# Routing's inverse by one-hots: the tile's one-hot moved to GpSimd, the weighted biases added by VectorE straight from PSUM

## The chip, the cores and the metric

One core of one Trainium2 chip runs the kernel. The metric is the device time of one launch in microseconds (us). The engines are named as in the profile: PE (TensorE), PEld (its weight loads), DVE (VectorE), ACT (ScalarE), POOL (GpSimd) and SP (SyncE, which only issues DMAs here).

## The reference, cut to what matters

A layer of attention with a post-layernorm, then a mixture of experts with a post-layernorm, for 4 x 1024 tokens of 256 numbers:

```python
x = _layernorm(x + attention(x, W_in, b_in, W_out, b_out))
raw_gate = softmax(x @ gate)                      # 16 experts
_, topk_idx = top_k(raw_gate, 3)
gate_topk = mask * raw_gate / max(sum(abs(mask * raw_gate)), 1e-12)
hidden = relu(x @ W1[e] + b1[e])                  # every expert e
expert_out = hidden @ W2[e] + b2[e]
x = _layernorm(x + sum_e gate_topk[e] * expert_out[e])
```

The part `sum_e gate_topk[e] * b2[e]` is the weighted bias of a token. It does not depend on the experts' matmuls and is added to `x` while the routing is worked out.

## The kernel before

Four stages run one after the other, each a block that begins and ends with a barrier of all engines: attention, routing (`routing_phase`), experts, combine. The change lies in routing alone.

Routing holds the 4096 tokens as `TILES` = 32 tiles of 128 rows in `x1`. After the layernorm and the gate, DVE picks the three experts of every token and works out, for each pair of a token and one of its `TOPK` = 3 experts, a slot: the slots of an expert are next to each other and filled up to tiles of 128, `SLOT_TILES` = 112 tiles in all. The expert stage gathers tokens by slot, so the map from pairs to slots has to be inverted. That is done with one-hot matrices on PE. For each of the 96 pairs of tile and choice (i = 3t + k):

- DVE compares the iota row `ioq` with `row_of` (the slot's row, per token): `row_hot`, 128 x 128 in bf16 (L1216).
- DVE compares the same iota with `tile_of` (the slot's tile) and multiplies with the token's row number plus 1, `part`: `tile_hot`, 128 x 112 in bf16 (L1218).
- ACT makes `row_hot_k`, that is `row_hot` times 4t + k + 1 (L1095).
- PE adds `row_hot`^T `tile_hot` into `inv_ps` (L1035) and `row_hot_k`^T `tile_hot` into a bank of `tr_ps` (L1038). Both sums run over all 96 pairs.

Each of the three one-hots has a ring of `HOT` = 8 buffers, handed back by PE through the semaphore `r_inv` (L1038). The rings lie in the memory of the tile `oh`, which is the name the profile gives them. Every sixth pair DVE also does one small instruction for `etile`, the expert of each slot tile (L1224, L1227). When all 96 pairs are done, DVE turns the two sums into the index lists `src_i` and `dst_i` (L1237 to L1252), and the barrier follows.

The weighted biases use the same engines. For each tile t, PE multiplies the gate weights `gT` with the 16 rows of `b2r` (32 rows of the array, f32, L1023) into one of two banks, `lg_ps` or `bb_ps` in turn. ACT copies the bank to `biases`, which lies in `xtt` (L1085), and POOL adds it to `x1` (L951). The first `EARLY_BIASES` = 10 tiles are done before the loop over the 96 pairs, on PE and ACT, while DVE works out the slots. The other 22 stand in the loop, one after every fourth pair.

What sets the order: each engine works through its own instructions in the order of the code, and semaphores tie them together. Nothing is scheduled by a program. Routing's stores of `x1` to memory (`r_stored`) must be done before `x1` is added to.

Of the kernel before, what the change touches and what calls it, by code (L numbers as in the profile page):

```python
# [7 lines left out]
ALU = mybir.AluOpType  # L8
# [9 lines left out]
B, T, D = 4, 1024, 256  # L18
# [803 lines left out]
def routing_phase(nc, A, dram, S):  # L822
# [5 lines left out]
    with ExitStack() as ctx:  # L828
        def sb(name, shape, dt):
# [6 lines left out]
        stats = sb("stats", [P, TILES, 6], F32)  # L836
        mv = sb("mv", [P, TILES, 2], F32)
        r = [sb(f"ln_{i}", [P, TILES], F32) for i in range(5)]
        EARLY_BIASES = 10
        HOT = 8  # L840
        LG = 8
        BY_POOL = 5
# [30 lines left out]
        unused = sb("unused", [P, SLOT_TILES], F32)  # L873
        ioq = sb("ioq", [P, P], BF16)

        biases = xtt[:, :, 0:D]
        g32 = xtt[:].rearrange("p a (t e) -> p (a t) e", e=32)
        ef = sb("ef", [1, SLOT_TILES], F32)
        eps = sb("eps", [P, 1], F32)
# [9 lines left out]
        inv_ps = ctx.enter_context(nc.psum_tensor("inv_ps", [P, 512], F32))  # L889
        bb_ps = ctx.enter_context(nc.psum_tensor("bb_ps", [P, 512], F32))  # L890
        x1_in = [ctx.enter_context(nc.semaphore(f"x1_in{b}")) for b in range(B)]
        names = ("r_slots r_ef r_oh r_oh_a r_oh_k r_bb_sb r_inv r_stored r_bb r_bbadd r_w r_small r_const r_chain "
                 "r_ln r_var r_std r_x1 r_xtr r_xtt r_lg r_lt r_lgt r_vo r_b1 r_bout r_bias_p r_bias_v r_rs r_sub "
                 "r_exp r_mask r_pre r_g32 r_gtr r_gt r_b2z r_b2").split()
        m = {k: ctx.enter_context(nc.semaphore(k)) for k in names}
# [23 lines left out]
        @block.gpsimd  # L919
        def _(pool):  # L920
            pool.memset(b2r[:], 0.0).then_inc(m["r_b2z"], 1)
            pool.memset(tri[:], 1.0).then_inc(m["r_const"], 1)
            pool.memset(ones[:], 1.0).then_inc(m["r_const"], 1)
            pool.memset(zero[:], 0.0).then_inc(m["r_const"], 1)
            pool.iota(io16[:], pattern=[[1, E_]], base=0, channel_multiplier=0,
                      allow_small_or_imprecise_dtypes=True).then_inc(m["r_const"], 1)
            pool.iota(iot[:], pattern=[[1, SLOT_TILES]], base=0, channel_multiplier=0,
                      allow_small_or_imprecise_dtypes=True).then_inc(m["r_const"], 1)
            pool.memset(onesf[:], 1.0).then_inc(m["r_const"], 1)
            pool.memset(ident[:], 0.0).then_inc(m["r_const"], 1)  # L930
            for t, pattern, base, mult in ((ioq, [[1, P]], 0, 0), (unused, [[P, SLOT_TILES]], PLACES * NTOK + P, 1),
                                           (part, [[0, 1]], 1, 1)):
                pool.iota(t[:], pattern=pattern, base=base, channel_multiplier=mult,
                          allow_small_or_imprecise_dtypes=True).then_inc(m["r_const"], 1)
            pool.wait_ge(m["r_const"], 10)
            pool.affine_select(out=ident[:], in_=ident[:], compare_op=ALU.not_equal, fill=1.0, base=0,
                               pattern=[[-1, P]], channel_multiplier=1).then_inc(m["r_const"], 1)

            pool.affine_select(out=tri[:], in_=tri[:], compare_op=ALU.is_gt, fill=0.0, base=0,
                               pattern=[[1, P]], channel_multiplier=-1).then_inc(m["r_const"], 1)  # L940

            pool.wait_ge(m["r_bout"], 1)
            for g in range(0, TILES, LG):
                pool.wait_ge(x1_in[g // LG], 16)
                for t in range(g, g + BY_POOL):
                    nc.gpsimd.tensor_tensor(x1[:, t, :], x1[:, t, :], bout[:], ALU.add).then_inc(m["r_bias_p"], 1)

            pool.wait_ge(m["r_stored"], 16 * TILES // LG)
            for t in range(TILES):
                pool.wait_ge(m["r_bb_sb"], t + 1)  # L950
                nc.gpsimd.tensor_tensor(x1[:, t, :], biases[:, t % 2, :], x1[:, t, :], ALU.add)\  # L951
                    .then_inc(m["r_bbadd"], 1)

        @block.tensor
        def _(pe):
# [62 lines left out]
            def weighted_biases(t):  # L1018

                if t >= 2:  # L1020
                    pe.wait_ge(m["r_bb_sb"], t - 1)
                r0 = 32 * (t % 4)
                nc.tensor.matmul((lg_ps, bb_ps)[t % 2][:, 0:D], gT[r0:r0 + 32, (t // 4) * P:(t // 4 + 1) * P],  # L1023
                                 b2r[r0:r0 + 32, :], start=True, stop=True).then_inc(m["r_bb"], 1)
# [6 lines left out]
                weighted_biases(t)  # L1031
            last = TOPK * TILES - 1
            for i in range(last + 1):
                pe.wait_ge(m["r_oh"], i + 1)
                nc.tensor.matmul(inv_ps[:, 0:SLOT_TILES], row_hot[:, i % HOT, :], tile_hot[:, i % HOT, :],  # L1035
                                 start=(i == 0), stop=(i == last), skip_group_check=True)
                pe.wait_ge(m["r_oh_k"], i + 1)
                nc.tensor.matmul(tr_ps[:, 0, 0:SLOT_TILES], row_hot_k[:, i % HOT, :],  # L1038
                                 tile_hot[:, i % HOT, :], start=(i == 0), stop=(i == last),
                                 skip_group_check=True).then_inc(m["r_inv"], 1)  # L1040
                if i % 4 == 0 and EARLY_BIASES + i // 4 < TILES:
                    weighted_biases(EARLY_BIASES + i // 4)

        @block.scalar
        def _(act):
            def take_logits(v):
                act.wait_ge(m["r_lg"], 2 * v + 2)
                if v >= 2:
                    act.wait_ge(m["r_lgt"], v - 1)
                nc.scalar.activation(lt_sb[v % 2][0:E_, :], lt_ps[v % 2][0:E_, :], ACT.Copy).then_inc(m["r_lt"], 1)  # L1050

            def take_transposes(u):

                act.wait_ge(m["r_xtr"], u + 1)
                if u >= 2:
                    act.wait_ge(m["r_lg"], u - 1)
                nc.scalar.activation(xtt[:, u % 2, :], tr_ps[:, u % 2, :], ACT.Copy).then_inc(m["r_xtt"], 1)
                if u >= 2 and u % 2 == 0:
                    take_logits(u // 2 - 1)

            for g in range(TILES // LG):

                ts = slice(g * LG, (g + 1) * LG)
                act.wait_ge(m["r_var"], g + 1)
                nc.scalar.activation(r[0][:, ts], mv[:, ts, 1], ACT.Sqrt, bias=eps[:, 0:1]).then_inc(m["r_std"], 1)
                act.wait_ge(m["r_rs"], g + 1)
                for t in range(g * LG, (g + 1) * LG):
                    nc.scalar.activation(x1[:, t, :], x1[:, t, :], ACT.Identity, bias=r[4][:, t:t + 1],
                                         scale=r[3][:, t:t + 1]).then_inc(m["r_x1"], 1)
                    if g >= 1 and t % 2 == 1:  # L1070
                        take_transposes((t - LG) // 2)
            for u in range((TILES - LG) // 2, TILES // 2):
                take_transposes(u)
            take_logits(TILES // 4 - 1)
            act.wait_ge(m["r_sub"], 1)
            nc.scalar.activation(prob[:], tmp[:], ACT.Exp).then_inc(m["r_exp"], 1)
            for u in range(2):
                act.wait_ge(m["r_gtr"], u + 1)
                nc.scalar.activation(gT[:, 512 * u:512 * u + 512], tr_ps[:, u, :], ACT.Copy).then_inc(m["r_gt"], 1)

            def take_biases(t):
                act.wait_ge(m["r_bb"], t + 1)
                if t >= 2:
                    act.wait_ge(m["r_bbadd"], t - 1)
                nc.scalar.activation(biases[:, t % 2, :], (lg_ps, bb_ps)[t % 2][:, 0:D], ACT.Copy)\  # L1085
                    .then_inc(m["r_bb_sb"], 1)

            for t in range(EARLY_BIASES):
                take_biases(t)
            for i in range(TOPK * TILES):  # L1090
                t, k = i // TOPK, i % TOPK
                act.wait_ge(m["r_oh_a"], i + 1)
                if i >= HOT:
                    act.wait_ge(m["r_inv"], i - HOT + 1)
                nc.scalar.activation(row_hot_k[:, i % HOT, :], row_hot[:, i % HOT, :], ACT.Copy,  # L1095
                                     scale=float(PLACES * t + k + 1)).then_inc(m["r_oh_k"], 1)
                if i % 4 == 3 and EARLY_BIASES + i // 4 < TILES:
                    take_biases(EARLY_BIASES + i // 4)

        @block.vector  # L1100
        def _(dve):
# [107 lines left out]
            V.tensor_copy(row_of[:], sloti[:, 1])  # L1209
            V.tensor_copy(tile_of[:], sloti[:, 2]).then_inc(m["r_slots"], 1)  # L1210
            dve.wait_ge(m["r_slots"], 1)
            for i in range(TOPK * TILES):
                t, k = i // TOPK, i % TOPK
                if i >= HOT:
                    dve.wait_ge(m["r_inv"], i - HOT + 1)
                V.tensor_scalar(row_hot[:, i % HOT, :], ioq[:], row_of[:, k, t:t + 1], None, ALU.is_equal)\  # L1216
                    .then_inc(m["r_oh_a"], 1)
                V.tensor_scalar(tile_hot[:, i % HOT, :], ioq[:, 0:SLOT_TILES], tile_of[:, k, t:t + 1],  # L1218
                                part[:, 0:1], ALU.is_equal, ALU.mult).then_inc(m["r_oh"], 1)
                if i % (TOPK * TILES // E_) == 0:  # L1220

                    e = i // (TOPK * TILES // E_)
# [422 lines left out]
```

## Time and profile before

| | us |
|---|---|
| median of 3 runs | 2046.22 |
| lowest and highest of them | 2040.72, 2048.99 |
| the profiled execution | 2043.57 |
| its span in the trace | 2041.8 |
| mean granted clock of PE over the span | 0.921 of full speed |
| the loop over the 96 pairs, first DVE start to last PE end | 1480.88 to 1533.01 |
| routing's last stretch, slots worked out to barrier | 1470.8 to 1538 |

The span is the time between the first and the last instruction in the trace, and the profiled execution's own time is 1.8 us longer. The busy tenths of the page show the three large stages: attention to about slice 27 of 40, routing in slices 28 to 30, experts and combine behind. PE busy time includes waiting in its pipeline, so a busy PE is not PE at its peak.

### The profile page before, as it was taken

To read this page: it belongs to the slowest core of one execution; us is meant where nothing else is said; L and a number is where in the kernel's file an instruction comes from. 1 tells how busy PE (TensorE), PEld (TensorE's weight loads), DVE (VectorE), ACT (ScalarE), POOL (GpSimd) and SP (SyncE) were. 2 spreads that over 40 slices of the span, in tenths; PEclk is the share of its full clock that TensorE was granted. 3 is DMA by queue.
4 is the path that set the end of the run, shared out by engine and by line. 5 is a ranking of instruction groups with operands and counts; after the bars stand their busy time and mean duration, and the time that the engine had idled before them with its cause. 6 is when DMAs were issued, how large, how long until landed. Compare 5 with 4: busy or idle time off the path is not lost. (4 is left out here: it accounts for less than half of the span.)

```text
span 2041.8 us, 37021 instructions
## 1 busy us (share of the span) xinstructions
PE 1796.5 (88%) x10191; PEld 1326.3 (65%) x10193; DVE 1403.8 (69%) x2857; ACT 763.1 (37%) x1691; POOL 1181.2 (58%) x1086
## 2 busy tenths in 40 slices
PE   4489999998998998999998999983598999999940
PEld 3366676666666765666675667642257999999940
DVE  3378878876886886887876887756694444444438
ACT  3134444443443443443443444433361222122225
POOL 2256776775676765766775677563134555555544
PEclk9689999998998998999999999996758999999975
DMA  9775566564555644654665456408601222222255
GB/s 319 243 203 146 154 187 177 156 188 136 153 171 156 192 147 144 194 159 136 184 174 161 125 164 186 126 1 300 217 1 55 72 69 69 70 71 70 70 174 186
DMA packets 164547, 301.36 MB, mean 148 GB/s; under 512 B 18768, under 2 KB 57360, under 8 KB 163360
## 3 DMA queue, kind: packets, MB, share of 16 engines
q1 hardware_dynamic: 152608, 269.79, 44.2%
q0 software_dynamic: 10752, 29.37, 4.6%
q8 instruction: 73, 1.20, 0.3%
q14 instruction: 90, 0.74, 0.1%
q10 hardware_dynamic: 1024, 0.26, 0.1%
HBM read 192.15 MB, written 106.95 MB: 146 GB/s over the span
## 5 line engine op out<-in xcount | busy, mean ns | idle before, releaser
L686 ACT ACTIVATE prob<-b_ps 128x512 f32<-128x512 f32 (+3 forms) x768 | 357.2, 489 | 443.4 <-PE b_ps L531 349.2
L454 POOL TENSOR_TENSOR acc<-acc,prob 128x1024 f32<-128x1024 f32 (+1 forms) x192 | 351.1, 1828 | 26.2 <-issue 22.7
L530 PE MATMUL b_ps<-q,k 128*128 128x512 f32 (+3 forms) x768 | 316.0, 416 | 36.2 <-issue 32.2
L755 DVE TENSOR_REDUCE max_b<-a_ps 128x1 f32<-128x512 f32 (+3 forms) x512 | 283.7, 570 | 87.3 <-PE a_ps L519 32.4
L427 POOL TENSOR_TENSOR roped<-rot 128x512 f32<-128x512 f32 x128 | 174.4, 1363 | 217.0 <-DVE rot L768 216.3
L519 PE MATMUL a_ps<-k,q 128*128 128x512 f32 (+3 forms) x768 | 276.4, 390 | 18.0 <-DMA k<-scratch_hilo 9.0
L604 PE MATMUL y_ps<-prob,v_sb 128*64 128x512 f32 (+3 forms) x1536 | 274.3, 492 | 0.0
L531 PE MATMUL b_ps<-q,k 65*128 65x512 f32 (+3 forms) x768 | 268.7, 354 | 0.0
L1410 DVE TENSOR_SCALAR hT<-h_ps,b1T 128x128 f32<-128x128 f32 x448 | 126.1, 344 | 190.7 <-PE h_ps L1329 171.6
L794 DVE RECIPROCAL inv<-inv 128x128 f32<-128x128 f32 x256 | 231.8, 927 | 7.7 <-ACT inv L718 7.0
L432 POOL TENSOR_TENSOR lo<-roped,hi 128x512 fp32r<-128x512 f32 x128 | 177.8, 1389 | 85.1 <-ACT hi L699 85.1
L1329 PEld LDWEIGHTS h_ps<-mxT,w_now 128*128 128x128 f32 x1792 | 219.0, 193 | 6.6 <-ACT mxT L1369 1.0
L604 PEld LDWEIGHTS y_ps<-prob,v_sb 128*64 128x64 f32 x1536 | 105.1, 137 | 180.6 <-issue 175.7
L1329 PE MATMUL h_ps<-mxT,w_now 128*128 128x128 f32 x1792 | 219.6, 276 | 0.6 <-ACT mxT L1369 0.6
L530 PEld LDWEIGHTS b_ps<-q,k 128*128 128x128 f32 x768 | 151.6, 197 | 94.8 <-issue 74.2
L1338 PE MATMUL yo_ps<-w,hT 128*128 x896 | 211.8, 379 | 0.0
L1303 POOL DMA_INDIRECT scratch_ys<-y,dst_i x112 | 110.8, 989 | 172.4 <-ACT y L1376 164.5
L511 PE MATMUL g_ps<-xT,w_sb 128*128 128x512 f32 x768 | 194.0, 403 | 9.6 <-DVE rot L768 6.6
L440 POOL TENSOR_SCALAR_AFFINE_SELECT prob<-prob 128x256 f32<-128x256 f32 x256 | 113.5, 449 | 149.5 <-ACT prob L686 147.1
L519 PEld LDWEIGHTS a_ps<-k,q 128*128 128x128 f32 x768 | 153.3, 200 | 42.3 <-DVE max_b L755 11.3
L511 PEld LDWEIGHTS g_ps<-xT,w_sb 128*128 128x128 f32 x768 | 147.9, 196 | 41.3 <-DVE rot L768 7.3
L1338 PEld LDWEIGHTS yo_ps<-w,hT 128*128 128x128 f32 x896 | 161.5, 190 | 17.4
(248 smaller groups left out, 2712.8 us busy)
## 6 DMA issues: line engine op xcount, KB each, us to landing
q<-scratch_hilo SPq DMA_DIRECT2D x192, 256.0 KB, 4.3
k<-scratch_hilo SPq DMA_DIRECT2D x192, 256.0 KB, 5.2
scratch_hilo<-hi SPq DMA_DIRECT2D x64, 512.0 KB, 4.1
scratch_hilo<-lo SPq DMA_DIRECT2D x64, 512.0 KB, 4.8
w_sb<-scratch_wsplit SPq DMA_DIRECT2D x32, 512.0 KB, 3.5
w<-in_L_ffn_W_dram SPq DMA_DIRECT2D x32, 512.0 KB, 10.4
got<-scratch_ys SPq DMA_DIRECT2D x32, 384.0 KB, 6.9
wv_sb<-scratch_wsplit SPq DMA_DIRECT2D x16, 512.0 KB, 6.3
```

What stands on the lines that cost most here:

```text
L432: nc.gpsimd.tensor_tensor(lo[:, half, cs], roped[:], hi[:, half, cs].bitcast(F32), ALU.subtract).then_inc(m["lo_done"], 1)
L454: nc.gpsimd.tensor_tensor(sums, old, probs(q), ALU.add).then_inc(m["sum_p"], 1)
L511: ins = nc.tensor.matmul(out, left, right, start=(a, b, k) == PRODUCTS[0], stop=(a, b, k) == PRODUCTS[-1], skip_group_check=True)
L519: ins = nc.tensor.matmul(out, q1[s][:, h, blk * P:(blk + 1) * P], k1[s][:, h, k0:k0 + w], start=True, stop=not diagonal, skip_group_check= ...
L530: nc.tensor.matmul(out, k1[s][:, h, js], q1[s][:, h, qs], start=True, stop=False, skip_group_check=True)
L531: ins = nc.tensor.matmul(out, k2[s][0:65, h, js], q2[s][0:65, half, h, 512 - w:512], start=False, stop=True, skip_group_check=True)
L604: ins = nc.tensor.matmul(y_ps[64 * h:64 * h + 64, 512 - w:512], v_sb[:, pairs, j, s, 64 * h:64 * h + 64], probs(q)[:, h, :], start=(j == 0 ...
L686: nc.scalar.activation(probs(q)[:, h, :], b_ps[:, h, 0:w], ACT.Exp).then_inc(exp_done[h], 1)
L755: nc.vector.tensor_reduce(out, a_ps[:, h, 0:w], AX_X, ALU.max, negate=True).then_inc(a_max[h], 1)
L794: nc.vector.reciprocal(part, part).then_inc(inv_done[c], 1)
L1329: ins = nc.tensor.matmul(h_ps[:, s, c * P:(c + 1) * P], w1_now[:, s, k, c * P:(c + 1) * P], xT[:, s, k * P:(k + 1) * P], start=(k == 0), s ...
L1338: ins = nc.tensor.matmul(yo_ps[:, s, 0:D], hT[:, s, c * P:(c + 1) * P], w2[:, bass.ds(e, 1), c, :].rearrange("p a d -> p (a d)"), start=(c ...
```

## The change

- POOL builds `tile_hot` (L952 of the changed kernel), with the same operations and ring as DVE did. It waits for `r_slots` once, and for its ring through `r_inv`. DVE keeps `row_hot` alone.
- DVE adds the weighted bias of tile t to `x1`, reading the bank in PSUM (L1207). It does so after `row_hot` of the tile's third pair (k = 2). ACT's copy and POOL's add of every tile are gone, and so is the semaphore `r_bb_sb` between them. PE now waits for the add (`r_bbadd`) before it writes a bank again.
- `EARLY_BIASES` goes from 10 to 2, and the other 30 stand in PE's stream one after every third pair.
- PE waits for both DVE's `row_hot` (`r_oh_a`) and POOL's `tile_hot` (`r_oh`) before the first of a pair's matmuls. The wait for the stores (`r_stored`) goes from POOL to DVE.

```diff
-        EARLY_BIASES = 10
+        EARLY_BIASES = 2
...
-            pool.wait_ge(m["r_stored"], 16 * TILES // LG)
-            for t in range(TILES):
-                pool.wait_ge(m["r_bb_sb"], t + 1)
-                nc.gpsimd.tensor_tensor(x1[:, t, :], biases[:, t % 2, :], x1[:, t, :], ALU.add)\
-                    .then_inc(m["r_bbadd"], 1)
+            pool.wait_ge(m["r_slots"], 1)
+            for i in range(TOPK * TILES):
+                t, k = i // TOPK, i % TOPK
+                if i >= HOT:
+                    pool.wait_ge(m["r_inv"], i - HOT + 1)
+                nc.gpsimd.tensor_scalar(tile_hot[:, i % HOT, :], ioq[:, 0:SLOT_TILES], tile_of[:, k, t:t + 1],
+                                        part[:, 0:1], ALU.is_equal, ALU.mult).then_inc(m["r_oh"], 1)
...
-                    pe.wait_ge(m["r_bb_sb"], t - 1)
+                    pe.wait_ge(m["r_bbadd"], t - 1)
...
             for i in range(last + 1):
+                pe.wait_ge(m["r_oh_a"], i + 1)
                 pe.wait_ge(m["r_oh"], i + 1)
...
-                if i % 4 == 0 and EARLY_BIASES + i // 4 < TILES:
-                    weighted_biases(EARLY_BIASES + i // 4)
+                if i % TOPK == TOPK - 1 and EARLY_BIASES + i // TOPK < TILES:
+                    weighted_biases(EARLY_BIASES + i // TOPK)
...
-            for t in range(EARLY_BIASES):
-                take_biases(t)
...
-                if i % 4 == 3 and EARLY_BIASES + i // 4 < TILES:
-                    take_biases(EARLY_BIASES + i // 4)
...
+            dve.wait_ge(m["r_stored"], 16 * TILES // LG)
+
+            def add_biases(t):
+                dve.wait_ge(m["r_bb"], t + 1)
+                V.tensor_tensor(x1[:, t, :], (lg_ps, bb_ps)[t % 2][:, 0:D], x1[:, t, :], ALU.add)\
+                    .then_inc(m["r_bbadd"], 1)
...
-                V.tensor_scalar(tile_hot[:, i % HOT, :], ioq[:, 0:SLOT_TILES], tile_of[:, k, t:t + 1],
-                                part[:, 0:1], ALU.is_equal, ALU.mult).then_inc(m["r_oh"], 1)
+                if k == 2:
+                    add_biases(t)
```

PE's stream where the loop begins, before (10 biases ahead of it, of which the last two are shown, then one after the first pair and one after the fifth; `inv_ps` and `tr_ps` are the two sums):

```order
1525 L1023 MATMUL lg_ps<-b2r,gT 128x256
1526 L1023 MATMUL bb_ps<-b2r,gT 128x256
1527 L1035 MATMUL inv_ps<-oh 128x112
1528 L1038 MATMUL tr_ps<-oh 128x112
1529 L1023 MATMUL lg_ps<-b2r,gT 128x256
1530 L1035 MATMUL inv_ps<-oh 128x112
1531 L1038 MATMUL tr_ps<-oh 128x112
1532 L1035 MATMUL inv_ps<-oh 128x112
1533 L1038 MATMUL tr_ps<-oh 128x112
1534 L1035 MATMUL inv_ps<-oh 128x112
1535 L1038 MATMUL tr_ps<-oh 128x112
1536 L1035 MATMUL inv_ps<-oh 128x112
```

The same place of PE's stream after the change:

```order
1517 L1024 MATMUL lg_ps<-b2r,gT 128x256
1518 L1024 MATMUL bb_ps<-b2r,gT 128x256
1519 L1037 MATMUL inv_ps<-oh 128x112
1520 L1040 MATMUL tr_ps<-oh 128x112
1521 L1037 MATMUL inv_ps<-oh 128x112
1522 L1040 MATMUL tr_ps<-oh 128x112
1523 L1037 MATMUL inv_ps<-oh 128x112
1524 L1040 MATMUL tr_ps<-oh 128x112
1525 L1024 MATMUL lg_ps<-b2r,gT 128x256
1526 L1037 MATMUL inv_ps<-oh 128x112
1527 L1040 MATMUL tr_ps<-oh 128x112
```

Only two biases are left ahead of the loop, and one follows every three pairs instead of every four.

DVE's stream some way into the loop, before (the two one-hots of each pair in turn, L1227 every sixth pair):

```order
778 L1218 TENSOR_SCALAR oh<-ioq,tile_of,part 128x112
779 L1227 SCALAR_TENSOR_TENSOR ef<-iot,cnt,ef 1x112
780 L1216 TENSOR_SCALAR oh<-ioq,row_of 128x128
781 L1218 TENSOR_SCALAR oh<-ioq,tile_of,part 128x112
782 L1216 TENSOR_SCALAR oh<-ioq,row_of 128x128
783 L1218 TENSOR_SCALAR oh<-ioq,tile_of,part 128x112
```

DVE's stream there after the change (L1214 is `row_hot`, L1207 the add of a weighted bias):

```order
778 L1207 TENSOR_TENSOR x<-bb_ps,x 128x256
779 L1214 TENSOR_SCALAR oh<-ioq,row_of 128x128
780 L1225 SCALAR_TENSOR_TENSOR ef<-iot,cnt,ef 1x112
781 L1214 TENSOR_SCALAR oh<-ioq,row_of 128x128 x2
782 L1207 TENSOR_TENSOR x<-lg_ps,x 128x256
783 L1214 TENSOR_SCALAR oh<-ioq,row_of 128x128 x3
784 L1207 TENSOR_TENSOR x<-bb_ps,x 128x256
```

The tile's one-hot of every pair is gone from it, and an add from PSUM came in after every third pair.

## Rows read from the trace of the kernel before

**Rows 1.** The page: span, busy times of the engines, and the granted clock in 40 slices

```profile
span 2041.8 us, 37021 instructions
PE 1796.5 (88%) x10191; PEld 1326.3 (65%) x10193; DVE 1403.8 (69%) x2857; ACT 763.1 (37%) x1691; POOL 1181.2 (58%) x1086
PEclk9689999998998998999999999996758999999975
```

**Rows 2.** Busy time by stretch: gate, early biases, the loop over pairs, tail

```profile
core 0: us, PE busy (x) PEld busy (x) DVE busy (x) ACT busy (x) POOL busy (x), PEclk, DMA share, GB/s
1420.50:1447.00 26.50, 23.79 (x137) 12.00 (x136) 6.49 (x32) 19.97 (x41) 0.00 (x0) 1.00 1.07 366
1469.40:1480.80 11.40, 8.72 (x20) 4.25 (x20) 10.75 (x22) 3.72 (x10) 9.08 (x10) 0.50 0.01 1
1480.80:1533.00 52.20, 50.95 (x236) 28.22 (x236) 52.05 (x211) 33.47 (x118) 16.35 (x22) 0.50 0.00 1
1533.00:1538.00 5.00, 0.01 (x1) 0.00 (x0) 3.81 (x14) 0.00 (x0) 0.00 (x0) 0.50 0.00 0
```

**Rows 3.** DVE's timeline in the loop: start us, duration us, instruction

```profile
1500.04 0.23 DVE L1216 TENSOR_SCALAR oh<-ioq,row_of 128x128 bf16<-128x128 bf16 x1
1500.20 0.29 DVE L1218 TENSOR_SCALAR oh<-ioq,tile_of,part 128x112 bf16<-128x112 bf16 x1
1500.42 0.32 DVE L1227 SCALAR_TENSOR_TENSOR ef<-iot,cnt,ef 1x112 f32<-1x112 f32 x1
1500.66 0.76 DVE L1216 TENSOR_SCALAR oh<-ioq,row_of 128x128 bf16<-128x128 bf16 x1
1501.35 0.29 DVE L1218 TENSOR_SCALAR oh<-ioq,tile_of,part 128x112 bf16<-128x112 bf16 x1
```

**Rows 4.** POOL's timeline there

```profile
1500.66 0.72 POOL L951 TENSOR_TENSOR x<-xtt,x 128x256 f32<-128x256 f32 x1 [1.35 <-ACT xtt L1085]
```

**Rows 5.** PE's timeline there, around one weighted bias

```profile
1500.83 0.27 PE L1038 MATMUL tr_ps<-oh 128*128 128x112 bf16 x1
1501.03 1.22 PE L1023 MATMUL bb_ps<-b2r,gT 32*128 32x256 f32 x2
1502.18 0.27 PE L1035 MATMUL inv_ps<-oh 128*128 128x112 bf16 x1
1502.25 0.30 PE L1038 MATMUL tr_ps<-oh 128*128 128x112 bf16 x1
1502.34 0.30 PE L1035 MATMUL inv_ps<-oh 128*128 128x112 bf16 x1
1502.44 0.30 PE L1038 MATMUL tr_ps<-oh 128*128 128x112 bf16 x1
```

**Rows 6.** DVE's timeline ahead of the loop, the slots

```profile
1471.76 1.11 DVE L1200 TENSOR_TENSOR inc<-inc,cnt 128x512 f32<-128x512 f32 x1
1473.98 0.72 DVE L1204 TENSOR_TENSOR gtmp<-slots,oh 128x512 f32<-128x512 f32 x1
1475.45 1.07 DVE L1204 TENSOR_TENSOR gtmp<-slots,oh 128x512 f32<-128x512 f32 x1
1479.11 0.58 DVE L1206 CAST sloti<-slotf 128x96 int32<-128x96 f32 x1
1479.72 0.65 DVE L1207 TENSOR_SCALAR sloti<-sloti 128x96 int32<-128x96 int32 x1
1480.29 0.20 DVE L1208 TENSOR_SCALAR sloti<-sloti 128x96 int32<-128x96 int32 x1
1480.88 0.26 DVE L1216 TENSOR_SCALAR oh<-ioq,row_of 128x128 bf16<-128x128 bf16 x1
```

**Rows 7.** Groups by line and form, DVE, the whole of routing: busy us, mean ns

```profile
L1201 DVE TENSOR_TENSOR slots<-pre_ps,inc 128x512 f32<-128x512 f32 x1 | 1.0, 1041 | 0.0
L1181 DVE TENSOR_TENSOR xtt<-gtmp,red 128x512 f32<-128x512 f32 x1 | 0.7, 692 | 0.0
L1155 DVE TENSOR_TENSOR gtmp<-lg_ps,red 128x512 f32<-128x512 f32 x1 | 0.7, 690 | 0.0
L1240 DVE TENSOR_TENSOR tot<-tr_ps,tot 128x112 f32<-128x112 f32 x1 | 0.3, 274 | 0.0
```

**Rows 8.** Groups by line and form in the loop, ACT

```profile
L1095 ACT ACTIVATE oh<-oh 128x128 bf16<-128x128 bf16 x96 | 28.9, 307 | 19.5 <-DVE oh L1216 17.6
```

**Rows 9.** PE's timeline at the loop's start and end

```profile
1481.42 0.27 PE L1035 MATMUL inv_ps<-oh 128*128 128x112 bf16 x1 [2.55 <-DVE oh L1218]
...
1532.73 0.28 PE L1038 MATMUL tr_ps<-oh 128*128 128x112 bf16 x1
```

**Rows 10.** Groups by line and form, POOL, the whole span

```profile
L440 POOL TENSOR_SCALAR_AFFINE_SELECT prob<-prob 128x256 f32<-128x256 f32 x256 | 113.5, 449 | 149.5 <-ACT prob L686 147.1 <-issue 2.5
L454 POOL TENSOR_TENSOR acc<-acc,prob 128x512 f32<-128x512 f32 x32 | 41.3, 1290 | 0.0
L454 POOL TENSOR_TENSOR acc<-acc,prob 128x256 f32<-128x256 f32 x32 | 23.3, 729 | 25.6 <-issue 22.7 <-POOL acc L454 1.4
L939 POOL TENSOR_SCALAR_AFFINE_SELECT tri<-tri 128x128 bf16<-128x128 bf16 x1 | 0.3, 292 | 0.0
```

More of the change, by code:

```diff
@@ L874, in routing_phase @@
         ioq = sb("ioq", [P, P], BF16)
-        biases = xtt[:, :, 0:D]
         g32 = xtt[:].rearrange("p a (t e) -> p (a t) e", e=32)
@@ L891, in routing_phase @@
         x1_in = [ctx.enter_context(nc.semaphore(f"x1_in{b}")) for b in range(B)]
-        names = ("r_slots r_ef r_oh r_oh_a r_oh_k r_bb_sb r_inv r_stored r_bb r_bbadd r_w r_small r_const r_chain "
+        names = ("r_slots r_ef r_oh r_oh_a r_oh_k r_inv r_stored r_bb r_bbadd r_w r_small r_const r_chain "
                  "r_ln r_var r_std r_x1 r_xtr r_xtt r_lg r_lt r_lgt r_vo r_b1 r_bout r_bias_p r_bias_v r_rs r_sub "
@@ L1079, in _ @@
                 nc.scalar.activation(gT[:, 512 * u:512 * u + 512], tr_ps[:, u, :], ACT.Copy).then_inc(m["r_gt"], 1)
[L1081 to L1086, printed above, removed]
-            for t in range(EARLY_BIASES):
-                take_biases(t)
             for i in range(TOPK * TILES):
```

## The prediction

> **What bounds the kernel now.** I read the page first. PE is busy 88% of the span, and its granted clock stands near full speed except in slices 27 to 30 [rows 1]. The change touches only that place, so I read busy time by stretch there [rows 2]. In the loop over the 96 pairs DVE is busy 52.05 of 52.20 us. PE shows 50.95 us, at a granted clock of 0.50, the lower of its two levels (1.2 GHz). The loop's end is what the tail, the barrier and the experts wait for, and nothing else runs meanwhile: DMA share is 0.00. So a microsecond of the loop is a microsecond of the kernel.
>
> DVE's timeline tells what DVE's 52 us are [rows 3]. The row's one-hot starts at 1500.04, the tile's at 1500.20 and the next instruction at 1500.42, so a pair costs 0.38 us, though the durations are 0.23 and 0.29. L1227 costs 0.24. Then a row's one-hot takes 0.76 us instead of 0.23. POOL's add began in the same moment and took 0.72 us [rows 4]. DVE went on at 1501.35, where 1500.82 would have been due: 0.53 us lost to one POOL instruction. The sum: 96 x 0.38 + 16 x 0.24 + 22 x 0.53 = 36.5 + 3.8 + 11.7 = 52.0 us, which is the loop.
>
> The second thing to see is how close PE is behind [rows 5]. Inside the catch-up a pair costs PE 2 x 0.093 us. Around a bias the step from the matmul before it to the matmul behind it is 1500.83 to 1502.18, that is 1.35 us. This is PE's own time: the tile's one-hot that the matmul at 1502.18 needs had started at 1501.35 and took 0.29 [rows 3], so it had been there for half a microsecond. Four pairs and a bias therefore take PE 1.35 + 0.07 + 6 x 0.093 = 1.98 us, against DVE's 4 x 0.38 + 0.67 x 0.24 + 0.53 = 2.21 us. PE has only 10% of slack, and the change alters the mix on PE too.
>
> **The change part by part.**
>
> *Ahead of the loop.* Ten POOL adds ran beside DVE's slot arithmetic (9.08 us of POOL busy) [rows 2]; they go. What they cost DVE is read from twins: L1200 took 1.11 us, L1181 of the same form 0.69 (0.42 lost); the second of the three L1204 took 1.07, as did the third, the first 0.72 (2 x 0.35); L1206 took 0.58 and L1207 0.65 where L1208 took 0.20 (0.38 and 0.45) [rows 6, 7]. That is 1.95 us. L1201 took 1.04; against L1155, which also reads PSUM, 0.35 too much, but its second input is strided, so 0 to 0.35. I take 2.1 us. The loop then starts at 1480.88 - 2.1 = 1478.8.
>
> *DVE in the loop.* The tile's one-hot leaves: 96 x 0.22 us. The adds come in: L1155 (512 columns, PSUM) takes 0.690 and L1240 (112 columns, PSUM) 0.274, which makes 1.04 ns a column and 0.42 us for 256 [rows 7]. Three pairs cost DVE 3 x 0.17 to 0.22, plus 0.42, plus half of 0.24: 1.05 to 1.2 us, 34 to 38 us for the loop, before any hold by POOL.
>
> *ACT.* 32 copies go and the 96 of L1095 at 0.307 us stay, 29.5 us [rows 8]. ACT was not the bound and is not after.
>
> *PE in the loop.* Eight biases move in from ahead of the loop, where PE had nothing else to do and DVE covered them; inside, that cover is gone. Three pairs and a bias cost 1.35 + 0.07 + 4 x 0.093 = 1.79 us by rows 5, and 1.68 us if half of the 0.20 us ahead of a bias (1500.83 to 1501.03) turns out to have been waiting. The added wait on `r_oh_a` costs PE nothing as long as DVE is ahead. DVE can be: its add of tile j waits for a bias that PE issued two groups earlier, and it still leaves six pairs of row one-hots ready.
>
> The end by PE's pace: the first three pairs are fed at the makers' speed. First matmul at 1478.8 + 0.5 (as now, 1480.88 to 1481.42 [rows 6, 9]), first bias in the loop, which waits for DVE's first add behind three one-hots and L1222, at about 1480.6 (3 x 0.22 + 0.24 + 0.42, and two holds by POOL of 0.2 each). Then 29 groups of 1.79 = 51.9, the last bias 1.15, and six pairs 1.0 + 0.3: the last matmul ends at 1534.9. Now it ends at 1532.73 + 0.28 = 1533.0 [rows 9]. That is **+1.9 us**; with 1.68 a group, -1.3 us.
>
> *POOL in the loop.* Its one-hot has no row in the trace. From below: one input, no pointer scalars, 0.292 us for 128 columns and 0.449 for 256, so 1.23 ns a column and 0.27 us for 112. From above, among rows of elementwise work: two inputs, 0.729 us for 256 and 1.290 for 512, so 2.19 ns a column and 0.41 us for 112 [rows 10]. It reads one stream but does two operations and two per-token scalars, so I take 0.4 and keep 0.27 to 0.75 (the whole 256-column add) for the range. PE asks for a pair every 1.79 / 3 = 0.60 us.
>
> POOL and DVE hold one another: rows 3 and 4 show DVE held for the POOL instruction's length less about 0.2. If a POOL one-hot of 0.4 and a row one-hot (0.17 from start to start) exclude one another wholly, a pair costs 0.57 us, just under PE's 0.60. By the Trainium skill (SBUF — State Buffer, "Who interferes with whom") the pair of ports that DVE and GpSimd share is an exclusive lock for the whole instruction, taken by a DVE tensor_scalar in a two-port mode and not by an instruction with one SBUF input outside these. By that rule the adds from PSUM run beside POOL unhindered; rows 3 and 4 agree for the one-hots, and no row shows a PSUM add beside POOL.
>
> *Tail.* L1237 to L1252 and the barrier stay as they are.
>
> The sum: 2043.57 + 1.9 = 2045.5 us for an execution like the profiled one, which lay 2.65 us below the median. Against the median I predict **2048.1 us**. The work off DVE is real (some 15 us) but PE, at the lower clock and with 30 biases in the loop in place of 22, takes it all.
>
> **The rivals.**
>
> 1. *POOL becomes the bound (slower).* Decides from 0.60 us a pair on, that is from 0.43 us for POOL's one-hot if the two engines exclude one another, from 0.60 if not. Each 0.1 us above is 9.6 us. At 0.75 us a pair: 1478.8 + 72 + 0.6 = 1551.4, +18 us, 2064.6. For it: the instruction has two operations and two pointer scalars that no POOL row has. Against it: both rows of elementwise work end below 0.45. The Trainium skill (GPSIMD Engine Reference, 3.1) speaks against the move: GpSimd is about half as fast as VectorE at elementwise work, and branching on data costs some 12 cycles an element. An estimate from that figure, if the comparison is done so, is 1.1 us for 112 elements, and the loop would be 107 us, about 55 us longer; no row here shows such a cost. Chance 0.17 for more than 10 us, and 0.10 for 0.60 to 0.70 a pair, +3 to +10 us.
>
> 2. *PE's clock rises (faster).* In the gate stretch PE stands at 1.00 (2.4 GHz) at 23.79 us busy of 26.50, but in the loop at 0.50 with 50.95 of 52.20 [rows 2]. Should it rise, a bias and pairs go at about half the price (0.9 us a group), and the makers bind: 0.40 to 0.57 us a pair, 38 to 55 us. At 0.45: 1478.8 + 43.2 + 0.6 = 1522.6, -10 us, 2036. Against it: what PE does between two biases hardly changes in kind, and it was as good as always busy at 0.50 before. Chance 0.06, of which half is faster by over 0.5%.
>
> 3. *A bias costs PE less than 1.35 us (faster).* If the step were mostly waiting that has another cause, PE would keep up with DVE and POOL and the loop would fall to 0.45 to 0.5 us a pair, -5 to -10 us. Rows 3 and 5 speak against it, since the one-hot was ready. Chance 0.05, of which 0.02 beyond 0.5%.
>
> **How the numbers follow.** A measurement of this kernel tells about 0.5%, 10.2 us, from no change. The forecast has 0.62. Slower by over 0.5%: 0.17. Faster by over 0.5%: 0.03 + 0.02, rounded to 0.05. Within: 0.78. The range: below, -1.3 us by the cheaper group, and part of rivals 2 and 3 and the spread of the median (2040.72 at the lowest of three), 2040. Above, rival 1 up to 0.72 us a pair, +15 us, 2062. Some 0.07 is left out below and 0.12 above.
>
> **What would show it.** The first row one-hot about 2 us after the last slot casts, at 1478.8 rather than 1480.9. What stood as L1200, L1206 and L1207 at 0.69, 0.21 and 0.20 us. In the loop PE's own row: bias to bias 1.8 us, PE's idle time before its matmuls near nothing, clock 0.50. POOL's one-hot about 0.4 us and idle between, released by PE. Loop 55 to 57 us long. The prediction is wrong if POOL's one-hot shows over 0.5 us with PE waiting for `r_oh`, if PE's clock shows 1.00 in the loop, or if bias to bias is under 1.6 us.

## Result and profile after

| | before | after |
|---|---|---|
| median, 4 runs each | 2045.38 | 2064.31 |
| lowest and highest | 2040.72, 2048.99 | 2063.03, 2068.65 |
| span of the profiled execution | 2041.8 | 2061.7 |
| loop, first DVE start to last PE end | 1480.88 to 1533.01: 52.1 us | 1480.41 to 1554.05: 73.6 us |

The ratio is 1.0098, with a 95% interval of 1.0072 to 1.0124. The change makes the kernel slower by about 19 us. The forecast was 2048.1 us in a range of 2040 to 2062, so the result lies outside it. It lies near what rival 1 had given for a POOL pace of 0.75 us a pair: 2064.6.

Busy time by stretch, the changed kernel (ahead of the loop, loop, tail), answers to [rows 2]:

```profile
core 0: us, PE busy (x) PEld busy (x) DVE busy (x) ACT busy (x) POOL busy (x), PEclk, DMA share, GB/s
1469.40:1480.40 11.00, 2.13 (x9) 1.01 (x7) 10.25 (x24) 1.20 (x2) 0.00 (x0) 0.50 0.00 0
1480.40:1554.00 73.60, 61.39 (x252) 29.12 (x252) 36.46 (x146) 25.32 (x96) 73.08 (x96) 0.50 0.00 1
1554.00:1559.00 5.00, 0.05 (x1) 0.00 (x0) 3.81 (x14) 0.00 (x0) 0.00 (x0) 0.50 0.00 0
```

DVE's share of the loop fell from 52.05 to 36.46 us, as planned. POOL is busy 73.08 of 73.60 us. The clock of PE is 0.50 as before.

Groups by line and form in the loop, answering to [rows 7, 8, 10] (busy us, mean ns, idle before):

```profile
L952 POOL TENSOR_SCALAR oh<-ioq,tile_of,part 128x112 bf16<-128x112 bf16 x96 | 73.1, 774 | 68.7 <-DVE tile_of L1201 68.7
...
L1214 DVE TENSOR_SCALAR oh<-ioq,row_of 128x128 bf16<-128x128 bf16 x96 | 22.8, 288 | 0.0
...
L1207 DVE TENSOR_TENSOR x<-bb_ps,x 128x256 f32<-128x256 f32 x16 | 6.8, 424 | 21.0 <-PE bb_ps L1024 21.0
```

POOL's one-hot takes 0.774 us in the mean, 0.737 in the median. The only idle time before it is the 68.7 us ahead of the first; in the loop it never waits. From the first start to the last it does one every 0.762 us. The add from PSUM takes 0.424 us, as worked out.

DVE's timeline ahead of the loop, answering to [rows 6]:

```profile
1473.32 0.69 DVE L1191 TENSOR_TENSOR inc<-inc,cnt 128x512 f32<-128x512 f32 x1
...
1476.54 0.69 DVE L1195 TENSOR_TENSOR gtmp<-slots,oh 128x512 f32<-128x512 f32 x1
...
1479.43 0.21 DVE L1197 CAST sloti<-slotf 128x96 int32<-128x96 f32 x1
1479.68 0.21 DVE L1198 TENSOR_SCALAR sloti<-sloti 128x96 int32<-128x96 int32 x1
```

All are free of POOL's hold, at the lengths of their twins. The instruction ahead of L1191 starts at 1472.60 here and at 1471.04 before, so this execution came to routing 1.56 us later; the loop started 0.47 us earlier all the same, a gain of 2.03 us.

PE's timeline at the loop's end, with what it waited for, answering to [rows 9]:

```profile
1551.51 0.25 PE L1037 MATMUL inv_ps<-oh 128*128 128x112 bf16 x1 [0.27 <-POOL oh L952]
1551.56 0.30 PE L1040 MATMUL tr_ps<-oh 128*128 128x112 bf16 x1
1552.26 0.25 PE L1037 MATMUL inv_ps<-oh 128*128 128x112 bf16 x1 [0.41 <-POOL oh L952]
1552.31 0.30 PE L1040 MATMUL tr_ps<-oh 128*128 128x112 bf16 x1
1552.99 0.25 PE L1037 MATMUL inv_ps<-oh 128*128 128x112 bf16 x1 [0.38 <-POOL oh L952]
1553.04 0.30 PE L1040 MATMUL tr_ps<-oh 128*128 128x112 bf16 x1
1553.71 0.25 PE L1037 MATMUL inv_ps<-oh 128*128 128x112 bf16 x1 [0.38 <-POOL oh L952]
```

DVE has made its last one-hot at 1549.1, and PE takes one pair each time POOL delivers one, every 0.72 to 0.75 us. Inside the loop the list of waits tells it otherwise, and could mislead (waiting engine, whom for, us in total, times, longest):

```profile
DVE x L1207 <- PE bb_ps L1024: 21.0, 15, 1.5
...
PE inv_ps L1037 <- POOL oh L952: 10.7, 5, 9.3
PE inv_ps L1037 <- DVE oh L1214: 9.7, 31, 0.5
```

By it DVE waits for PE most (34.8 us with the 13.8 us of the other bank), PE waits for DVE 31 times, and for POOL only five times. PE now waits for two semaphores before a pair, and the profile names the one that came last. DVE, which is held back by its ring until PE has taken a pair, makes its next one-hot just after; that is a consequence of POOL's pace, or else it is the cause. Two theories had to be told apart.

- **Theory 1:** POOL's pace, 0.76 us a pair, sets the loop.
- **Theory 2:** the hand-overs between PE's biases and DVE's adds set it, and POOL only looks busy.

### The profile page after: what moved, and what is told of

It reads as the page before. It is cut to its first block and busy times, and to the rows that moved or that the text cites. A ratio compares the mean times of both kernels' runs of the same rounds, so it can differ in the third digit from the quotient of the medians.

```text
span 2061.7 us, 37056 instructions
## 1 busy us (share of the span) xinstructions
PE 1801.1 (87%) x10192; PEld 1325.2 (64%) x10193; DVE 1388.2 (67%) x2793; ACT 754.2 (37%) x1659; POOL 1229.8 (60%) x1150
## 5 line engine op out<-in xcount | busy, mean ns | idle before, releaser
L519 PEld LDWEIGHTS a_ps<-k,q 128*128 128x128 f32 x768 | 152.9, 199 | 43.5 <-DVE max_b L755 11.4
```

The costliest lines, as they stand in the source:

```text
L519: ins = nc.tensor.matmul(out, q1[s][:, h, blk * P:(blk + 1) * P], k1[s][:, h, k0:k0 + w], start=True, stop=not diagonal, skip_group_check= ...
```

## Experiments

Loop lengths below are from the first start of the row's one-hot on DVE to the end of PE's last matmul. PE's modelled end is its last start plus 0.3 us. Where a second time is given with "against", it is the kernel before, run again beside the experiment.

**The biases of the loop left out** (`e4`). The matmuls of PE and the adds of DVE for tiles 2 to 31 are left out, so the output lacks these biases.

```diff
-                if i % TOPK == TOPK - 1 and EARLY_BIASES + i // TOPK < TILES:
-                    weighted_biases(EARLY_BIASES + i // TOPK)
...
-                if k == 2:
+                if k == 2 and t < 2:
                     add_biases(t)
```

> The changed kernel without the 30 weighted biases of the loop (PE's matmuls and DVE's adds for tiles 2 to 31 are left out, so the output lacks them). Theory 1, POOL's pace of 0.76 us a pair sets the loop: it stays at 73 to 74 us. Theory 2, the hand-overs between PE's biases and DVE's adds set it, as the list of waits names them (DVE waits for PE 34.8 us in the loop): PE has only 0.19 us a pair left, and the loop falls to 45 us or less.

Measured: 2064.64 us in one run, loop 1480.2 to 1551.9, 71.7 us. The stretch in the trace:

```profile
1480.20:1551.90 71.70, 33.17 (x192) 13.04 (x192) 30.02 (x117) 29.14 (x96) 71.09 (x96) 0.50 0.00 1
```

PE lost nearly half of its busy time and DVE a fifth, and the loop kept POOL's length. Theory 2 falls. The 1.9 us that it did lose are POOL's: its start to start went from 0.762 to 0.741 us in the mean.

**Only the other part of the change: DVE builds both one-hots, POOL nothing** (`e1`).

```diff
-                pe.wait_ge(m["r_oh_a"], i + 1)
...
+                V.tensor_scalar(tile_hot[:, i % HOT, :], ioq[:, 0:SLOT_TILES], tile_of[:, k, t:t + 1],
+                                part[:, 0:1], ALU.is_equal, ALU.mult).then_inc(m["r_oh"], 1)
```

(and POOL's loop gone)

> One part of the change alone: DVE adds the biases from PSUM as in the changed kernel, with 2 early biases and 30 in the loop, but DVE also builds the tile's one-hot as before, and POOL does nothing. DVE's sum: 96 x 0.38 + 16 x 0.24 + 32 x 0.36 = 51.8 us with no hold by POOL; PE's pace by the prediction's sum 1.79 us a group, 53.7. Theory 1 (POOL alone made it slow): loop 53 to 56 us, time within 3 us of the kernel before. Theory 2 (the biases in the loop and DVE's adds made it slow): loop over 65 us, time 10 us or more above before.

Measured: 2047.84 us against 2043.83, ratio 1.0016 (0.9998 to 1.0033); loop 1479.5 to 1536.5, 57.0 us. Busy time in that stretch:

```profile
1479.50:1536.50 57.00, 56.34 (x252) 31.19 (x252) 53.41 (x242) 29.68 (x96) 0.00 (x0) 0.50 0.00 1
```

Theory 1 holds: without POOL's one-hot the loss of 1% is gone, and PE is the one that is busy throughout.

**POOL builds every second pair's tile one-hot** (`e2`).

```diff
+                if not (i % 2 == 0):
+                    continue
                 nc.gpsimd.tensor_scalar(tile_hot[:, i % HOT, :], ...
...
+                if i % 2 == 0:
+                    pe.wait_ge(m["r_oh_a"], i + 1)
+                    pe.wait_ge(m["r_oh"], i // 2 + 1)
+                else:
+                    pe.wait_ge(m["r_oh_d"], (i + 1) // 2)
```

(DVE builds the others and counts them on `r_oh_d`)

> The changed kernel, with POOL building the tile's one-hot only of every second pair and DVE that of the others. POOL then needs 48 x 0.76 = 37 us, DVE 96 x 0.17 + 48 x 0.22 + 4 + 11.5 = 42 us, so neither binds. Theory 1: the loop falls from 73.6 us to what PE's pace gives, 1.79 us a group of three pairs and a bias, 54 to 55 us in all; this measures the PE term of the prediction. If PE's step around a bias were partly waiting, 1.68 a group or less, it is 51 us or less. Theory 2 (hand-overs): stays over 65 us.

Measured: 2046.71 us, ratio 1.0011 (0.9995 to 1.0026); loop 1478.8 to 1536.3, 57.5 us. PE's timeline from one bias to the next:

```profile
1504.78 1.22 PE L1026 MATMUL bb_ps<-b2r,gT 32*128 32x256 f32 x2
1505.93 0.27 PE L1042 MATMUL inv_ps<-oh 128*128 128x112 bf16 x1
1505.99 0.30 PE L1045 MATMUL tr_ps<-oh 128*128 128x112 bf16 x1
1506.09 0.30 PE L1042 MATMUL inv_ps<-oh 128*128 128x112 bf16 x1
1506.18 0.30 PE L1045 MATMUL tr_ps<-oh 128*128 128x112 bf16 x1
1506.27 0.30 PE L1042 MATMUL inv_ps<-oh 128*128 128x112 bf16 x1
1506.37 0.30 PE L1045 MATMUL tr_ps<-oh 128*128 128x112 bf16 x1
1506.60 1.22 PE L1026 MATMUL lg_ps<-b2r,gT 32*128 32x256 f32 x2
```

1506.60 - 1504.78 = 1.82 us, with no wait in it, in every group that I read (the first bias starts at 1481.12, the last, 29 groups on, at 1533.90), and the same in the run with DVE alone. This is PE's pace that the forecast rested on (1.79). The 0.2 us ahead of a bias is there although nothing is awaited: 0.23 from 1506.37 to 1506.60. The loop is longer than the 54 to 55 us expected for this run, which were rounded down from the prediction's own sum, 1478.8 to 1534.9 = 56.1 us. It is 1.4 us longer than that sum: 0.03 x 29 = 0.9, and 0.5 at the start, where the first bias came 2.3 us after the loop's begin (1481.12), not 1.8.

**What POOL's 0.74 us consists of** (`m1`, and `m3` for widths). POOL gets extra instructions on scratch tiles in the 68.7 us in which it waits for the slots, four of each form, each waited for. `m1` has eight forms:

```diff
+            for _ in range(4):
+                nc.gpsimd.tensor_scalar(jb[:, 0:56], ioq[:, 0:56], part[:, 0:1], part[:, 0:1], ALU.is_equal, ALU.mult).then_inc(m["r_junk"], 1)
+                pool.wait_ge(m["r_junk"], JUNK())
```

> The changed kernel with 32 extra POOL instructions, four of each of eight forms, each waited for, on scratch tiles in the 68 us in which POOL waits for the slots. The kernel's time should not change by more than 1 us, since POOL is idle there for 68.7 us. Question: what of the 737 ns of POOL's one-hot is what. Theory A, pointer scalars cost: the forms with immediates take about 0.3 us, the one with two per-token scalars 0.74, the one with one about 0.5. Theory B, the second operation costs: one-operation forms about 0.3 to 0.4 whatever the scalars. Theory C, the comparison costs (a branch or a select per element): add and multiply with the same scalars about 0.4, all comparing forms near 0.7. Theory D, a fixed price of the instruction: 56 columns take nearly the 0.74 us of 112. If it is all per column, 56 columns take about 0.43.

Measured: 2065.27 us in one run. Each line below gives the shortest, the median and the longest of its four instructions in ns. A per-token scalar is a value that the instruction reads from memory for each row, as the one-hot reads `tile_of` and `part`; a constant stands in the instruction. L956: compare, then multiply, two per-token scalars; L974 the same in f32; L959 on 56 columns; L965 the same with two constants; L971 add and multiply, two per-token scalars; L962 compare alone, one per-token scalar; L968 compare alone with a constant; L977 multiply alone with a constant.

```profile
L956 POOL TENSOR_SCALAR jb<-ioq,part x4: 737/738/754, 1411.9 to 1414.4; 128x112 bf16<-128x112 bf16 x4
L974 POOL TENSOR_SCALAR jf<-iot,part x4: 737/738/743, 1428.8 to 1431.4; 128x112 f32<-128x112 f32 x4
L959 POOL TENSOR_SCALAR jb<-ioq,part x4: 552/574/1097, 1415.2 to 1417.8; 128x56 bf16<-128x56 bf16 x4
L965 POOL TENSOR_SCALAR jb<-ioq x4: 587/588/592, 1421.1 to 1423.1; 128x112 bf16<-128x112 bf16 x4
L971 POOL TENSOR_SCALAR jb<-ioq,part x4: 428/434/1050, 1426.1 to 1428.3; 128x112 bf16<-128x112 bf16 x4
L962 POOL TENSOR_SCALAR jb<-ioq,part x4: 560/561/562, 1418.4 to 1420.4; 128x112 bf16<-128x112 bf16 x4
L968 POOL TENSOR_SCALAR jb<-ioq x4: 486/488/524, 1423.7 to 1425.5; 128x112 bf16<-128x112 bf16 x4
L977 POOL TENSOR_SCALAR jb<-ioq x4: 487/488/497, 1432.2 to 1433.9; 128x112 bf16<-128x112 bf16 x4
```

Two forms have one instruction of about twice the length of the other three. Both ran beside adds of DVE with two inputs from SBUF (the output bias onto `x1`). The third of L959 started at 1416.60, the first of L971 at 1426.08:

```profile
1416.27 1.08 DVE L1151 TENSOR_TENSOR x<-x,bout 128x256 f32<-128x256 f32 x3
1425.90 1.09 DVE L1151 TENSOR_TENSOR x<-x,bout 128x256 f32<-128x256 f32 x3
```

So the means of these two forms (0.699 and 0.586 us) mislead, and the medians are read here.

The comparison is the largest single item. With the one-hot's two per-token scalars, compare and multiply takes 0.74 us (L956) and add and multiply 0.43 (L971), so theory C's "about 0.4" for the add came true, and the comparison costs 0.30 us more. It does not do so everywhere: alone and with a constant, a compare takes what a multiply does, 0.49 us (L968, L977), so "all comparing forms near 0.7" is wrong. Theory A falls as the whole cause, since the add with two per-token scalars is the cheapest form of all; so does theory B, since that form has two operations. Among the comparing forms a per-token scalar adds 0.07 us (L962 over L968), and a multiply behind it 0.10 (L965 over L968). Half the columns save 0.18 us (L959 under L956), so theory D holds in part: three quarters of the time stay at 56 columns. Why the comparison is dear together with a second operation and two per-token scalars, and not alone, these runs do not show.

`m3` has other widths and kinds:

> The changed kernel with POOL instructions of other widths and kinds on scratch tiles in its idle stretch, four of each: the one-hot's operations over 336 and 224 columns; tensor_tensor adding over 112 and 336 columns and multiplying over 112, all bf16. From the first look at forms, 0.74 us at 112 columns and 0.70 at 56 make 0.77 ns a column and a fixed 0.66 us: 336 columns should take 0.91 us and 224 0.83. If the fixed part belongs to tensor_scalar alone, tensor_tensor at 112 columns takes 0.41 us by the slope of the prediction (2.19 ns a column), and 0.9 at 336.

Measured: 2068.61 us in one run, whose routing began some 5 us later than in the changed kernel's; its loop is 73.1 us long. L958 and L961 are the one-hot's operations, L967 and L964 tensor_tensor adding, L970 multiplying (shortest, median and longest in ns):

```profile
L958 POOL TENSOR_SCALAR jb<-jc,part x4: 1484/1492/1610, 1414.9 to 1419.7; 128x336 bf16<-128x336 bf16 x4
L961 POOL TENSOR_SCALAR jb<-jc,part x4: 1110/1112/1112, 1421.4 to 1425.0; 128x224 bf16<-128x224 bf16 x4
L967 POOL TENSOR_TENSOR jb<-jc x4: 758/784/884, 1428.0 to 1430.7; 128x336 bf16<-128x336 bf16 x4
L970 POOL TENSOR_TENSOR jb<-jc x4: 372/372/434, 1431.5 to 1433.0; 128x112 bf16<-128x112 bf16 x4
L964 POOL TENSOR_TENSOR jb<-jc x4: 371/371/372, 1426.2 to 1427.6; 128x112 bf16<-128x112 bf16 x4
```

The 0.91 us expected at 336 columns was wrong because it came from the mean of the 56-column form, with its one long instruction. By the shortest of each width, 0.552, 0.737, 1.110 and 1.484 us at 56, 112, 224 and 336 columns, the one-hot's form costs 3.3 ns a column throughout and 0.37 us besides. tensor_tensor costs 0.37 us at 112 columns, near the 0.41 that the prediction had worked out as its bound from above. The one-hot's tensor_scalar costs twice that; a tensor_scalar that adds and multiplies, 0.43, does not. A tensor_tensor that compares was planned as well (`m2`), but no run shows one.

**POOL and DVE side by side** (`e6`): half the tile one-hots on POOL, and the loop's biases left out as in `e4`, so the output lacks them.

> The kernel with the tile's one-hot shared half and half between POOL and DVE, without the 30 weighted biases of the loop (PE's matmuls and DVE's adds of tiles 2 to 31 are left out). It shows what the one-hots alone cost. DVE: 96 x 0.165 + 48 x 0.22 + 16 x 0.24 = 30.2 us, POOL 48 x 0.75 = 36 us. If the two engines run side by side, the loop is 36 to 38 us, POOL's; if POOL's instruction holds DVE for its length less 0.2 us, as the 128x256 add did in the kernel before, DVE needs 30 + 48 x 0.55 = 56 us and the loop is over 50.

Measured: 2028.75 us in one run, loop 1477.7 to 1518.4, 40.7 us. Busy time in that stretch:

```profile
1477.70:1518.40 40.70, 25.53 (x192) 15.41 (x192) 35.08 (x164) 26.39 (x96) 39.88 (x48) 0.50 0.01 1
```

Groups by line and form there:

```profile
L954 POOL TENSOR_SCALAR oh<-ioq,tile_of,part 128x112 bf16<-128x112 bf16 x48 | 39.9, 844 | 68.6 <-DVE tile_of L1204 68.6
...
L1217 DVE TENSOR_SCALAR oh<-ioq,row_of 128x128 bf16<-128x128 bf16 x96 | 23.4, 286 | 3.5 <-PE tr_ps L1045 2.3
```

The two run nearly side by side. DVE's row one-hot takes 0.286 us in the mean beside POOL's one-hot, where the 256-column add had made it 0.76 [rows 3, 4]. POOL pays more: its one-hot goes from 0.74 to 0.844, which makes the loop longer than the 36 to 38 us expected. Its last two instructions, which start when DVE has done its last one-hot, take 0.737 us each. By the Trainium skill (SBUF — State Buffer, "Who interferes with whom") the lock would be held for the whole instruction. The trace agrees with that for the add (0.72 us of POOL, 0.53 lost by DVE), but not for this one-hot: POOL was busy 39.88 of the 40.70 us, and DVE made 144 one-hots in them. What sets the two cases apart (POOL's operation, its number of inputs, its type) is not shown.

**Biases in twos.** Ahead of the loop of the kernel before, and nowhere inside it, biases stand directly one after another, and there two were done 1.2 us after they began. So the loop's biases are issued two at a time, in the kernel with half on POOL (`e3`), with all on DVE (`e7`), and with a third on POOL (`e8`).

```diff
-                if i % TOPK == TOPK - 1 and EARLY_BIASES + i // TOPK < TILES:
-                    weighted_biases(EARLY_BIASES + i // TOPK)
+                if i % 6 == 5 and EARLY_BIASES + i // 3 < TILES:
+                    weighted_biases(i // 3 + 1)
+                    weighted_biases(i // 3 + 2)
```

> The kernel with the tile's one-hot shared between POOL and DVE (every second pair each), and the weighted biases of the loop issued two at a time after every sixth pair instead of one after every third. In the run before, PE's step from bias to bias was 1.82 us in each group and set the loop, 57.5 us. Two biases back to back use different row groups of the array: ahead of the loop in the kernel before, the first two were both done 1.2 us after they began. Theory 1 (PE's price per bias binds): six pairs and two biases cost PE about 1.1 + 1.6 us in place of 3.6, and the loop falls to DVE's pace, 44 to 48 us; with the 2 us ahead of the loop the time is 6 to 10 us below the kernel before. Rival: two biases in a row cost twice one, nothing changes, loop 57 us.

Measured: 2039.3 us against 2043.59, ratio 0.9983 (0.9972 to 0.9995); loop 1481.9 to 1531.3, 49.4 us. PE's timeline:

```profile
1503.62 0.79 PE L1026 MATMUL lg_ps<-b2r,gT 32*128 32x256 f32 x1
1503.63 0.79 PE L1026 MATMUL bb_ps<-b2r,gT 32*128 32x256 f32 x1
1504.21 0.63 PE L1026 MATMUL lg_ps<-b2r,gT 32*128 32x256 f32 x1
1504.22 0.63 PE L1026 MATMUL bb_ps<-b2r,gT 32*128 32x256 f32 x1
1504.78 0.27 PE L1042 MATMUL inv_ps<-oh 128*128 128x112 bf16 x1
```

A bias is two records in this view, in `e2` shown as x2. The two biases start 0.01 us apart, and the next matmul starts at 1504.78, 1.16 us after them: two cost what one did (1.15 in the run `e2`). Their operands lie in different groups of 32 rows (`r0` = 32 * (t % 4)); no run has two in the same group, so whether that is needed is open. The time fell by 3.5 to 4.3 us, less than the expected 6 to 10, since the loop took 49.4 us, not 44 to 48. None of the three engines was busy throughout: PE 43.1, DVE 43.5 and POOL 39.4 us of the 49.4. What holds this loop is open.

> As the kernel in which DVE builds both one-hots and adds the biases from PSUM (POOL idle), with the biases of the loop issued two at a time after every sixth pair. Theory 1: PE no longer binds, DVE does at 96 x 0.38 + 16 x 0.24 + 32 x 0.34 = 51.2 us; loop 51 to 53 us instead of 56.9, time about 2 us below the kernel before, because the loop starts 2 us earlier. Rival (two biases cost PE twice one): loop 57 us again.

Measured: 2042.69 us, ratio 0.9999 (0.9985 to 1.0012); loop 1479.2 to 1530.7, 51.5 us. The loop is as expected, so the overlap of two biases helps without POOL too (57.0 us in `e1`). The time is no different from before within 0.15%, 3 us, which leaves room for the 2 us expected.

> As the kernel with POOL and DVE sharing the tile's one-hot and the biases in twos, but with POOL building only every third pair's instead of every second's. POOL: 32 x 0.8 = 26 us; DVE: 96 x 0.165 + 64 x 0.22 + 16 x 0.24 + 32 x 0.34 = 44.7 us and small holds. With half on POOL the loop was 49.4 us, with neither of DVE, PE and POOL always busy. If POOL's late one-hots cost there, the loop is now 46 to 48 us; if DVE's own sum is what counts, 50 to 51. Either way within 2 us of that kernel's time and 2 to 6 us below the kernel before.

Measured: 2037.78 us against 2042.68, ratio 0.9970 (0.9960 to 0.9981); loop 1479.1 to 1527.6, 48.5 us, between the two cases, so these are not told apart. DVE was busy 48.54 of the 50 us from 1478 to 1528, and POOL's one-hot took 0.92 us in the mean. This is the fastest version: 0.3% below the kernel before.

## Why the prediction was wrong

- *What bounds the kernel before:* DVE's loop, PE close behind. Right. With POOL out of the way PE set the loop at 1.82 us a group (1.79 forecast), and the kernel came out 2 to 4 us above before (`e1` and `e2`; neither is clear of no change), where the forecast for a PE-bound loop had said +1.9. (The page's granted clock is low in slices 2, 39 and 40 as well, not only in 27 to 30; they lie outside the change.)
- *Ahead of the loop:* 2.1 us saved, 2.03 measured. Right, and so were the twins it was read from. L1201's extra 0.35 us was not POOL's: it takes 1.01 us without POOL, so 0.03 of it at most. Its strided input may be the reason; no run varies that.
- *The adds from PSUM:* 0.42 us forecast, 0.424 measured, and not hindered by POOL: none of the 32 took over 0.426, and in `e1`, where POOL does nothing, they took 0.42.
- *PE's clock* (rival 2) stayed at 0.50 in every kernel here, at 33 as at 61 us of PE busy in the loop. *A cheaper bias* (rival 3) did not come by itself; it came from the order, in `e3`.
- *POOL's one-hot is the step that failed.* "I take 0.4" us, and it is 0.74 by itself and 0.77 in the loop, so POOL gives a pair every 0.76 us where PE asks for one every 0.60 and sets the loop. The bound of 0.41 from above came from rows of tensor_tensor adds, and the two operations and the two per-token scalars were added to it at no price. For an add and a multiply with two per-token scalars that is about right, 0.43 us (`m1`, L971). What was put at nothing is the comparison: in this form it costs 0.30 us more. The rest of the bound held: tensor_tensor takes 0.37 us at 112 columns. No tensor_scalar of POOL stood in the trace before, and the affine select that gave the bound from below is a different instruction. The range of this unknown had 0.75 in it, but the time's range stopped at 0.72. The prediction's own sign of being wrong, over 0.5 us with PE waiting for `r_oh`, is what the trace shows.
- *The mutual hold* was allowed for in full, at 0.17 us a pair. It is smaller for this instruction: at the loop's end, when DVE is done, a pair comes every 0.72 to 0.75 us, and over the whole loop every 0.762. By these numbers a one-hot of 0.4 us would have stayed under PE's 0.60; no run shows one.
- *Rival 1* had the mechanism, the threshold (0.60 us a pair) and the price right: 1551.4 for the loop's end at 0.75 a pair, 1554.05 measured at 0.76. It had 0.17 of the chance. That its 2064.6 lies 0.3 us from the measured median is in part luck: this execution's loop ended 2.65 us later than the rival said (it came to routing 1.56 us later, and 0.76 for 0.75 makes 1.1), and what lies behind the loop was 1.1 us shorter and the execution nearer to its median than the one before. The Trainium skill (GPSIMD Engine Reference, 3.1) puts GpSimd at half of VectorE's speed for elementwise work, by an add of two inputs of 2048 columns. Here the one-hot takes 0.22 us from DVE's stream [rows 3] and 0.76 of POOL's, so 3.5 times as much. Its figure for branching on data, an estimate of 1.1 us for this one-hot, is not borne out: it takes 0.74, and a lone compare costs what a multiply does.

## What to carry to other kernels

Before work moves to an engine, find a row of that very instruction, with its operations and operand kinds, on that engine; a neighbouring instruction of the same width is no bound, and here one operation changed for another made 0.43 us into 0.74. If there is none, put a few of it into an idle stretch of that engine and read them one by one: one that another engine held up can turn a mean, and the conclusion with it. And when a semaphore list shows two engines waiting for each other while a third is busy without a gap, look at the end of the loop, where the others have run out of work: the last steps show the pace-maker.

## What the runs showed of the hardware

- POOL's tensor_scalar, 112 columns: 0.49 us for one operation with a constant, 0.43 for add and multiply with two per-token scalars, 0.74 for compare and multiply with the same. The last costs 3.3 ns a column and 0.37 us besides, from 56 to 336 columns. tensor_tensor at 112 columns takes 0.37.
- A POOL tensor_tensor add of 256 columns held DVE's one-hots for 0.53 us. In `m1` a POOL tensor_scalar beside DVE's adds with two inputs from SBUF took 0.5 to 0.6 us longer than its twins. POOL's one-hot of 0.84 us slowed DVE's row one-hot by 0.05 in the mean and was itself 0.1 longer; DVE's adds from PSUM took 0.424 us beside POOL and 0.42 without it.
- Two biases (f32 matmuls on 32 rows each), in different row groups and back to back, cost PE as much as one, 1.16 us at a granted clock of 0.50. Between matmuls on 128 rows each of them costs that alone, and 0.23 us ahead of it.
